# Softmax reciprocals through scratch memory, products on POOL, and separate places for the first and the last batch

## The reference

```
q = LN(x) @ Wq.T + bq;  k, v = ctx @ Wk.T + bk, ctx @ Wv.T + bv   # 32 heads of 16 channels, 8 groups of keys
w = softmax(mask(q @ k.T / 4));  att = w @ v
x = x + tanh(g_xattn) * (att @ Wo.T + bo)
h = LN(x)
x = x + tanh(g_ffn) * ((silu(h @ gate) * gs * (h @ up) * us) @ down) * ds   # 512 -> 1536 -> 512
```

## Time and profile before

| | |
|---|---|
| three runs | 639.71, 639.89, 640.62 us (median 639.89) |
| the profiled execution | 643.64 us, of which 640.6 us are its span |
| mean granted TensorE clock | 0.931 of full speed |
| busy in the span | PE 576.8, DVE 512.8, ACT 361.7, POOL 236.6 us |
| instructions | 14331 |

### The profile page before, as it was taken

The page is one execution under the profiler, slowest core; times in us unless marked ns, Lnnn a source line. Parts: engine busy times, 40 slices in busy tenths (PEclk is TensorE's granted clock), DMA queues, the critical chain, the costliest instruction groups (busy, mean ns, idle before and its releaser), DMA issues.

```text
span 640.6 us, 14331 instructions
## 1 busy us (share of the span) xinstructions
PE 576.8 (90%) x5133; PEld 362.6 (57%) x5133; DVE 512.8 (80%) x1543; ACT 361.7 (56%) x672; POOL 236.6 (37%) x321
## 2 busy tenths in 40 slices
PE   3683686779999999999999999999998999899697
PEld 3661352337665676567755775577644753574483
DVE  3678989899998999999999998998898897444321
ACT  3532676537674577457844675467635763672261
POOL 3202002030565037512743084307540654166174
PEclk9976686589999999999999999999997999799699
DMA  8573826332222222313140313021302011002000
GB/s 284 172 252 116 237 85 199 108 69 67 65 57 59 76 60 83 71 49 85 37 118 27 104 32 93 27 64 38 94 19 58 4 52 35 17 3 67 0 17 33
DMA packets 53871, 50.22 MB, mean 78 GB/s; under 512 B 7501, under 2 KB 41386, under 8 KB 53802
## 3 DMA queue, kind: packets, MB, share of 16 engines
q1 hardware_dynamic: 53280, 48.72, 26.6%
q10 hardware_dynamic: 522, 0.61, 0.3%
HBM read 35.15 MB, written 9.44 MB: 70 GB/s over the span
## 4 chain that ended last, share of the span: by engine, by line
PE 77%; DVE 13%; issue 4%; POOL 2%; ACT 2%; DMA 1%; SPq 0%; ACTq 0%; POOLq 0%; DVEq 0%
PE work L1003 28%; PE work L1014 11%; PE av L903 9%; PE work L934 6%; DVE junk L724 6%; PE sc L883 5%; PE work L981 5%; PE sc L893 5%; DVE ws L736 3%; PE work L943 1%; PE work L990 1%; PE work L954 1%; PE work L964 1%; PE work L920 1%; DMA padc_u<-in_mask_BxS_bk 1%
## 5 line engine op out<-in xcount | busy, mean ns | idle before, releaser
L724 DVE CUSTOM_DVE_ANT_0 junk<-sc,mq 128x256 bf16<-128x256 f32 x512 | 186.0, 420 | 19.7 <-PE sc L883 18.7
L736 DVE SCALAR_TENSOR_TENSOR ws<-sc,padc,mask_k 128x1024 f32<-128x1024 f32 x128 | 163.9, 1281 | 18.3 <-PE sc L893 17.3
L590 ACT ACTIVATE ws<-ws 128x1024 f32<-128x1024 f32 x128 | 133.7, 1053 | 29.6 <-DVE ws L736 29.6
L528 POOL TENSOR_TENSOR ff<-ga,up 128x256 f32<-128x256 f32 x96 | 69.5, 728 | 166.7 <-DVE ga L817 159.1
L1003 PE MATMUL work<-h_h,wg 128*128 128x256 f16 x384 | 92.3, 280 | 3.0 <-DVE h_l L812 3.0
L1003 PE MATMUL work<-h_l,wg 128*128 128x256 f16 x384 | 91.7, 278 | 0.0
L1003 PE MATMUL work<-h_h,wu 128*128 128x256 f16 x384 | 91.3, 277 | 0.0
L1003 PE MATMUL work<-h_l,wu 128*128 128x256 f16 x384 | 91.2, 277 | 0.0
L883 PE MATMUL sc<-ks,qs 48*128 48x256 f16 x512 | 55.5, 293 | 20.8 <-DVE mx L724 20.8
L903 PE MATMUL av<-ws,va 128*32 128x256 f32 x1024 | 73.7, 408 | 0.5 <-ACT ws L590 0.5
L535 POOL TENSOR_TENSOR f_l<-ff,f_h 128x256 f16<-128x256 f32 x96 | 64.4, 683 | 26.4 <-ACT f_h L656 26.4
(11 more groups left out here) (124 smaller groups left out, 997.2 us busy)
## 6 DMA issues: line engine op xcount, KB each, us to landing
qs<-q_scratch SPq DMA_DIRECT2D x96, 64.0 KB, 2.4
cin<-in_ctx SPq DMA_DIRECT2D x8, 512.0 KB, 4.3
xin<-in_x SPq DMA_DIRECT2D x8, 512.0 KB, 4.8
xb<-in_x SPq DMA_DIRECT2D x8, 512.0 KB, 3.8
att_u<-un SPq DMA_DIRECT2D x128, 32.0 KB, 2.0
out_x<-yt SPq DMA_DIRECT2D x16, 256.0 KB, 2.2
ks<-k_scratch SPq DMA_DIRECT2D x48, 64.0 KB, 3.7
q_scratch<-qh SPq DMA_DIRECT2D x16, 128.0 KB, 1.9
```

What stands on the lines that cost most here:

```text
L528: pool.tensor_tensor(ff[:, n % RING, :], ga[:, n % RING, :], up[:, n % RING, :], ALU.mult).then_inc(ff_done, 1)
L590: act.activation(ws[:, unit, :, :], ws[:, unit, :, :], ACT.Exp, scale=1.0 / SSC).then_inc(exp_done, 1)
L724: last = dve.tensor_tensor_reduce(junk[:, HPG * t + j, :], sc[0][:, place(j)], mq[b % 2][:, t, :], 1.0, -3.4e38, ALU.add, ALU.max, mx[:, t ...
L736: dve.scalar_tensor_tensor(out=ws[:, n % 4, :, :], in0=sc[1][:, :].rearrange("p (j l) -> p j l", j=HPG), scalar=padc[b % 2][:, kt:kt + 1], ...
```

## The change

The four steps that follow the sums are replaced. The constant `spread` and its matmuls go. `den` becomes 128 partitions of 64, one `reciprocal` on DVE works on all of it, and a new piece `bounce` on SP writes the result to scratch memory and, when that has landed, reads it back with 8 DMAs, each repeated on 16 partitions, into `rd`. A new piece `mul[0,1]` on POOL multiplies `att_u` by `rd`. To make each head's sums contiguous, `un` is written in another order, and `gather` copies pieces twice as long. The factor 64 comes from the ones, which are now 1/64. Three small tiles lie in others' room. Every place of every table is new, and the first and the last batch have a table of their own for all pieces.

```diff
-    "spread": [35.39, 39.286],
...
+    "mul": [93.1907, 93.4096],
...
+    "bounce": [-41.3952],
...
-def order(table, first, more=()):
+def order(table, first, last, more=()):
...
+            of_batch = first.get(name, row) if b == 0 else last.get(name, row) if b == NB - 1 else row
+            places += [(at + STEPS * b, name, n, b) for n, at in enumerate(of_batch)]
...
-        den, rden = sb("den", [H, L], f32), sb("rden", [H, L], f32)
-        rd = sb("rd", [2 * H, L], f16)
+        den, rden = sb("den", [P, H * L // P], f32), sb("rden", [P, H * L // P], f32)
+        rd = sb("rd", [P, KT, L], f32)
...
-                        sp.dma_start(den[G * j:G * j + G, :],
+                        sp.dma_start(den[32 * j:32 * (j + 1), :],
                                      un[32 * j + HD:32 * j + HD + 1, :, :]).then_inc(den_in, 16)
+                if name == "bounce":
+                    sp.wait_ge(recip_done, b + 1)
+                    past(sp, rd_in, 128 * b)
+                    sp.dma_start(d_dram.rearrange("(p l) -> p l", p=P), rden[:, :]).then_inc(rd_out, 16)
+                    sp.wait_ge(rd_out, 16 * (b + 1))
+                    past(sp, att_done, 2 * b)
+                    for gp in range(2):
+                        rows = d_dram.rearrange("(j f k l) -> f j k l", j=HPG, f=2, k=KT)[gp]
+                        for j in range(HPG):
+                            at = 64 * gp + HD * j
+                            sp.dma_start(rd[at:at + HD, :, :],
+                                         rows[j:j + 1].broadcast_to([HD, KT, L])).then_inc(rd_in, 16)
...
-                                         un[32 * j:32 * j + HD, 4 * n + gp:4 * n + 4:2, :]).then_inc(att_in[n], 16)
+                                         un[32 * j:32 * j + HD, g:g + 2, :]).then_inc(att_in[n], 16)
...
+                if name == "mul":
+                    pool.wait_ge(rd_in, 128 * (b + 1))
+                    pool.wait_ge(att_in[n], 128 * (b + 1))
+                    past(pool, at_ready, 2 * (b - 1) + n + 1 if b else 0)
+                    pool.tensor_tensor(att[:, 2 * n:2 * n + 2, :], att_u[:, 2 * n:2 * n + 2, :],
+                                       rd[:, 2 * n:2 * n + 2, :], ALU.mult).then_inc(att_done, 1)
...
-                    act.activation(un[:, n, :], av[:, 0:L], ACT.Copy).then_inc(un_ready, 1)
+                    act.activation(un[:, KT * (n % 2) + n // 2, :], av[:, 0:L], ACT.Copy).then_inc(un_ready, 1)
...
                 if name == "recip":
                     dve.wait_ge(den_in, 64 * (b + 1))
+                    past(dve, rd_out, 16 * b)
                     dve.reciprocal(rden[:, :], den[:, :]).then_inc(recip_done, 1)
-                    dve.wait_ge(recip_done, b + 1)
-                    if b:
-                        wait_ready(dve, "spread", 1, b - 1)
-                    dve.tensor_scalar(rd[0:H, :], rden[:, :], SA, None, ALU.mult).then_inc(rd_high, 1)
-                    dve.wait_ge(rd_high, b + 1)
-                    dve.scalar_tensor_tensor(out=rd[H:2 * H, :], in0=rden[:, :], scalar=SA, in1=rd[0:H, :],
-                                             op0=ALU.mult, op1=ALU.subtract).then_inc(rd_ready, 1)
-                if name == "spread":
-                    wait_ready(dve, name, n, b)
-                    dve.wait_ge(att_in[n], 128 * (b + 1))
-                    dve.tensor_tensor(att[:, 2 * n:2 * n + 2, :], halves(bank), att_u[:, 2 * n:2 * n + 2, :],
-                                      ALU.mult).then_inc(freed, 1)
...
-                if name == "spread":
-                    if n == 0:
-                        pe.wait_ge(rd_ready, b + 1)
-                    bank, ready = work_bank(name, n, b)
-                    for i in range(2):
-                        last = mm(bank[:, L * i:L * (i + 1)], spread[:, 2 * n + i, :], rd[:, :], start=True,
-                                  stop=True)
-                    last.then_inc(ready, 1)
```

More of the change, by code:

```diff
@@ L52 @@
 PE_AT = {
[L53 to L60, removed]
@@ new lines @@
+    "scores": [-3.849, -2.3639, -0.6236, 0.9274, 2.3879, 3.3987, 6.7873, 9.1658, 13.6988, 15.6473, 17.6495, 19.3542,
+               22.2306, 23.4977, 26.2235, 27.7632],
+    "weighted": [1.1512, 5.5644, 12.727, 16.9294, 19.3967, 23.3099, 27.9378, 30.07],
+    "mrow": [-6.3968, 7.6428],
+    "xT": [-56.9243, -54.6982],
+    "cT": [-51.5662, -51.3942],
+    "x2T": [48.0239, 48.7259],
+    "q": [-50.2048, -46.7554],
+    "out": [41.7576, 42.9403],
+    "down_a": [66.842, 69.6159],
+    "down_b": [70.9311, 72.2213],
@@ L70 @@
+    "k": [-44.5672],
+    "v": [-29.03],
 }
 ACT_AT = {
[L73 to L83, removed]
@@ new lines @@
+SP_FIRST = {
+    "load_xb": [-81.4541],
+    "put_q": [-125.9395, -118.633],
+    "get_q": [-119.2254, -117.0761],
+    "rows": [-86.6616, -68.931],
+    "gather": [-53.7151, -44.1337],
+    "store": [15.9447, 25.2649],
+    "put_k": [-9232.4829],
+    "get_k": [-120.5604],
+    "den": [-45.9496],
+    "bounce": [-41.3356],
+}
+PE_LAST = {
+    "gu": [45.1695, 45.6329, 49.5713, 55.5486, 56.4787, 57.3278, 57.5477, 58.9958, 60.4438, 60.6575, 61.0849,
+           61.1917],
+    "maxima": [-24.1323, -23.3559, -21.9553, -19.7465, -17.3152, -14.0356, -10.9786, -9.3392, -6.8783, -4.2665,
+               -3.3183, -0.1222, 0.7523, 4.6621, 5.7298, 7.0469],
+    "scores": [-2.125, -1.5864, -0.3569, 0.7248, 1.7465, 4.046, 6.8718, 9.0241, 15.7599, 15.7625, 15.766, 16.7416,
+               17.4024, 19.0811, 21.111, 22.2265],
+    "weighted": [1.7521, 6.989, 15.6758, 15.7608, 16.9178, 19.1623, 23.7767, 26.3907],
+    "mrow": [-4.3804, 8.7852],
+    "xT": [-57.1331, -57.0172],
+    "cT": [-51.9353, -50.8368],
+    "x2T": [43.4163, 44.7062],
+    "q": [-48.4003, -45.0209],
+    "out": [38.3091, 38.801],
+    "down_a": [61.2452, 61.2986],
+    "down_b": [66.9563, 68.8422],
+    "k": [-45.9787],
+    "v": [-18.7871],
+}
@@ new lines @@
+POOL_LAST = {
+    "pad_row": [28.1259],
+    "padc": [27.9055],
+    "power": [-17.6638, 90.147],
+    "mrow": [46.1164, 67.9966],
+    "split_att": [88.6835, 88.9758],
+    "add_y": [174.1084, 174.2907],
+    "add_bo": [74.5573],
+    "fuse": [91.0128, 91.8787, 100.0991, 100.256, 102.5103, 149.8359, 150.3986, 152.2684, 161.5662, 168.0035,
+             170.2807, 170.5628],
+    "fsplit": [93.9471, 98.3638, 149.1441, 149.2654, 153.6425, 157.6043, 166.1235, 170.3512, 170.4218, 170.5158,
+               171.0582, 171.1307],
+    "mul": [87.8089, 88.308],
+}
```

326 lines of the change are left out of this document (211 added, 115 removed).

## The result

The changed kernel takes 648.3 us (median of 4, 645.84 to 651.37) where the kernel before took 640.25 on the same chip: ratio 1.0117, interval 1.0062 to 1.0173. Timed once more later, it took 646.13 us against 642.45, ratio 1.0059, interval 1.0037 to 1.0080. So it is slower, by 1.2% in the first measurement and 0.6% in the second, with both intervals above 1, and not 7.9 us faster. The profiled execution took 647.84 us with a span of 646.1; the span before was 640.6.

What follows compares the result with a forecast made beforehand. It took DVE to set the pace before 138 us, PE to bound the middle, and PE gaps to cost time after 478. Gains of 1.3 + 2.6 + 4 = 7.9 us gave a median of 632.0 us, range 621 to 643.

Steps and rivals of the forecast that it cites:

- Middle, "does the chain stay hidden?": Between `weighted[7]` and `out[0]` of a middle batch, 26 us of PE work hide the chain by some 3 us.
- rival 3: Slower: the chain from the sums to `out` shows in every batch, 667 us or 646 by its length; chance 0.12.
- First stage: Up to `out[0]` of batch 0, DVE the bound: 3.8 + 1 - 3.5 = 1.3 us gained.
- the delay of 3.5: First stage: `out[0]` 2 to 3.6 us late behind the chain, `get_k` of batch 2 late at once; 3.5 us taken.
- I take 1: First stage: batch 1's projections between the maxima save 1 us of DVE's 12.2 us of idle time.
- Middle, PE's work: Over 8 batches, 5.1 us of `spread` saved less about 2.5 for more blocks: 2.6 us gained, bounds none and 5.1.
- End: After 478 us, three gaps on PE gain 2 + 1 + 1 = 4 us.
- the third gap: Behind the last `weighted`, up to `gu` of batch 7: 8.15 us lost before, 6.8 now; 1 us gained, from -3 to 6.
- (a): `out` of batch 0 starts about 1 us earlier than 138.2, PE or DVE in front of it waiting for DMA.
- (b): Batch period 66.5 to 66.7 us, PE without gaps, no wait of `out` or `scores` for POOL or DMA.
- (c): A gap of 2.5 to 4 us ahead of the last `out`, none between it and `x2T`.
- (d): Durations: the reciprocal 0.5 us, the products 1.2, the write 1.9 to landing.

Runs made afterwards that it cites:

- The two runs with the edit both ways: Changed kernel with batch 0's feed forward at a middle batch's places: 639.21 us; kernel before with batch 0's last three `down` pieces behind `out[1]` of batch 1: 647.9 us.
- the write twice: Changed kernel with batch 0's feed forward at the middle batches' places, plus the write of `rden` issued and awaited twice in every batch: 648.46 us, ratio 1.0087.

## Why the prediction was wrong

**Middle, "does the chain stay hidden?": the step that failed.** The span went from 640.6 to 646.1 us: 2.0 lost up to the first `out[0]`, 8.1 from there to `out[0]` of batch 2, 1.2 to that of batch 5, and 5.9 gained behind it. The 8.1 us belong to this step, for which the sum had 2.6 us gained in 8 batches. I counted PE's pieces between `weighted[7]` and `out[0]` in a middle batch and took the count for all. The first batch had got a table of its own, and in it `down_a[1]`, `down_b[0]` and `down_b[1]` stand behind `out[1]` of batch 1. I had looked at the new tables at the start and at the end, not at what batch 0's table does to batch 1's period. The two runs with the edit both ways settle its price:

| batch 0 to batch 2, us | down early | down late |
|---|---|---|
| old chain | 134.3 | 140.2 |
| new chain | 135.2, 134.3 | 142.4, 141.7 |

The late pieces cost 5.9 us with the old chain and 6.5 to 8 with the new one (less the half clock at the start of the window, about 4.7 and 6.5). That is the loss from batch 0 to 2; the mechanism is not the one that I had feared (rival 3, a bare chain in each batch), and the one that I first formed (a bare chain in batch 1) is at most a part of it. PE work was put off from a period in which DVE holds PE up without it, into one in which PE is the bound. How the loss reaches PE differs: with the old chain all of PE's waits but 0.2 us are for DVE. In the changed kernel about half of the loss, 2.0 us of waiting and 1.8 of half clock behind it, hangs on `ks`, which comes late behind `bounce`, and 1.9 us of the waits are for DVE. Since the old chain loses most of it without that, the longer chain adds some 2 us in the net. Why I had missed it: the sum priced the stages by durations and gaps that were there, and had no term for work that changes its stage. With the pieces early, the middle stays hidden as I said: from batch 1 to batch 4 the periods are 66.9 to 67.2 us, and no `out` waits.

**First stage: 1.3 us gained by my sum, 2.0 lost in this pair of profiles, nearer to 4 in the mean** (`out[0]` at 136.2 in three profiles of the old stream, 140.0 in six of the new). Two units of `maxima` less ahead of `den` (2.9 us) and 1 us less idle time put `den` at 118.49 - 2.9 - 1 = 114.6 us in my sum, and the walk puts `out[0]` 22.4 us behind it (the cover of 18.9 and the delay of 3.5), at 137.0. The second number came true, 140.21 - 117.86 = 22.35 us (before 19.75), but by luck. The chain was as long as walked: `at_l` was done at 139.1, 21.2 us behind the start of `den`, for 20.9 to 22.5. But `out[0]` did not wait for it or for `ks`, so the delay of 3.5 us that I charged was not there; no wait of PE or DVE in this stretch names POOL or a DMA. DVE had 19.6 us of work in it (my cover was 18.9), and stood 4.1 us for PE's scores (before 1.9), with a granted clock of 0.58 (before 0.67):

```profile
DVE junk L885 <- PE sc L1033: 2.1, 2, 1.5
DVE ws L897 <- PE sc L1043: 2.0, 2, 1.4
```

The early row of 4.8 us for a write did not come true: this one, of 32 KB, landed in 1.7. The about 2.0 us of the Trainium skill (DMA: Bandwidth & Descriptors, Anatomy of one DMA) were nearer, though that section is about DMAs that GpSimd issues, and these are SP's.

The loss itself lies ahead of `den`. It started at 117.86, only 0.6 us earlier than before, although the two units had gone from there (25 of 27 are left). The term "I take 1", for the projections between the maxima, was mis-sized: from 34.5 us to `den` DVE was idle for 83.99 - 72.51 = 11.5 us before and for 83.36 - 69.22 = 14.1 in the changed kernel, 2.6 us more instead of 1 less.

```profile
34.50:118.49 83.99, 57.46 (x487) 28.56 (x486) 72.51 (x270) 42.59 (x58) 8.75 (x14) 0.72 0.59 175
```

```profile
34.50:117.86 83.36, 56.49 (x480) 30.40 (x482) 69.22 (x248) 42.56 (x61) 11.28 (x16) 0.73 0.54 157
```

The largest single wait: `q[0]` of batch 1 came behind all of the first eight maxima, at half clock, and DVE stood:

```profile
59.29 0.42 DVE L885 CUSTOM_DVE_ANT_0 junk<-sc,mq 128x256 bf16<-128x256 f32 x1 [3.85 <-PE sc L1033]
```

No run changes these places alone, so which of them costs it stays open. In the write twice PE does wait there, 1.1 us for `ks` and 2.1 at the next `mrow`, and `out[0]` starts 0.5 us later behind `den`, so in the first batch the chain is covered by about 1 us.

**Middle, PE's work: 2.6 us by my sum, under 1.** The price of `spread` was mis-sized: 0.32 is what the pair takes on the chain at the end, with nothing beside it; 0.22 in a row of others. 0.43 a batch saved less 0.3 for three more blocks would leave 0.13, but the periods from batch 2 to 4 went from 67.17 and 66.90 to 66.87 and 67.14, so 0.03; where the other 0.1 went stays open. From batch 4 to 5 it was 66.0 before and 66.0 to 67.2 now, although `v` (1.3 us of PE's work) has left that period.

**End: 4 us by my sum, 5.9 gained** (from `out[0]` of batch 5 to the end 168.1 before, 162.2 now). The walk of the third gap held: `out[0]` of batch 7 started 21.8 us after the last `weighted` ended (573.12 + 1.04), for 22 to 23.7, after a gap of 2.3 us; the gap behind `out[1]` is gone, `gu` began 0.1 us behind `h_l`, at full clock (1.00 in the last window, 0.90 before). But this gap gained 4.1 us, where I took 1. From the last `weighted` to `gu` of batch 7 are 35.84 us, and by the prediction's durations PE's work in them is 14.3 + 10.4 + 5.3 + 1.8 = 31.8: 4.0 lost for 8.15 before. I had 6.8, because I put 2 us down for `out` at half clock; the clock stayed full:

```profile
574.16:610.00 35.84, 30.99 (x208) 19.91 (x207) 10.59 (x23) 15.89 (x38) 19.36 (x26) 1.00 0.11 25
```

The first two gaps gained the other 1.8 us, for the 3 that I took.

Of the signs, (a) came out the other way: `out[0]` of batch 0 was 2.0 us later, and PE in front of it waited for DVE's maxima, 1.6 and 0.9 us, and not for a DMA. (b) failed in batch 1, and behind batch 2 PE had no gaps and nothing waited, but the period was 66.9 to 67.1 and not 66.5 to 66.7. (c) held, with 2.3 us for 2.5 to 4. Of (d) the reciprocal took 0.55 us (0.5), the products 1.27 (1.2, the row of `at_l` gave 1.16), and the write landed in 1.6 to 2.3, with a median of 1.6 (1.9). Chance: I gave slower 0.16, nearly all for a chain that is 4 us longer than counted. The chain was as long as counted; the time came out slower for another reason.

## What to carry to other kernels

When a change has an order of its own for the first or the last round, count the pieces of each stretch in that round, not in a middle one. Work that is put off is free only if the engine that leaves it can use the time; look at the second engine's busy time in that stretch (here 60.9 us of DVE under a period that was to be 59.6).

When a stage is priced by the start of one instruction, write down the times that the sum implies on the way to it. Here `den` at 114.6 us shows at once where the loss lies (117.9 for 114.6). And compare the wait, not only the number: the 22.4 us behind it came out as 22.35, with another wait than the one forecast.

Issue time on a queue and landing time are two things: merging 8 DMAs into 2 took 2.3 us off the queue and put some 9 on the landing (from the last issue to the products 11 us for 2).

## What the runs showed of the hardware

- The same 512 KB from DRAM, repeated on 16 partitions each, took 5.4 us from first issue to use as 8 DMAs and 12.4 us as 2 whose slowest dimension is 4, with 9.7 and 3.9 packets of 4096 bytes under way at a time.
- A matmul of 64 partitions by 256 columns cost 0.11 us between others, where the pair alone suggested 0.16.
- Behind a wait of 2.0 us PE's granted clock was at its lower level for 3.7 us, which cost 1.8 us more (changed kernel, 205.2 to 208.9 us). Behind PE's shorter waits between 191 and 199 us of the kernel before with the late pieces, none over 1 us, it stayed full (1.00 from 138.3 to 200.1).
- The old stream reached `out[0]` of batch 0 at 134.7, 135.8 and 138.2 us in three profiled executions, without an edit ahead of it but for doubled `spread` in one. One profile of before is therefore no measure of 2 us in the first stage, where PE's clock changes level several times; the six profiles of the new stream without an edit in its chain lay between 138.9 and 140.6.
